# Row maxima of attention scores, reduced one head or two heads at a time

## The reference

```python
def attn(x, Wq, bq, Wk, bk, Wv, bv, Wo, bo):       # 32 heads of 16
    q, k, v = heads(x @ Wq + bq), heads(x @ Wk + bk), heads(x @ Wv + bv)
    probs = softmax(einsum('bhqd,bhkd->bhqk', q, k) / sqrt(16))
    return merge(einsum('bhqk,bhkd->bhqd', probs, v)) @ Wo + bo
def ffn(x, gate_w, up_w, down_w, gate_scale, up_scale, down_scale):   # 512 -> 1536 -> 512, weights rounded to fp8
    return qmm(silu(qmm(x, gate_w, gate_scale)) * qmm(x, up_w, up_scale), down_w, down_scale)
x = x + layernorm(attn(layernorm(x)))
x = x + layernorm(ffn(layernorm(x)))
```

## Time and profile before

| | |
|---|---|
| median of 3 runs | 1727.8 us (1726.58 to 1728.24) |
| the profiled execution, its own time | 1726.27 us |
| its span, first to last instruction | 1724.5 us |
| PE busy | 1584.0 us (92%) |
| DVE busy | 1192.2 us (69%) |
| ACT busy | 907.9 us (53%) |
| POOL busy | 600.8 us (35%) |

### The profile page before, as it was taken

How to read it: one execution, slowest core, us unless ns; L and a number is a source line. 1 busy time by engine, 2 the same in 40 slices (tenths; PEclk the granted TensorE clock), 3 DMA queues, 4 the chain that set the end, 5 groups by cost and what they waited for, 6 DMA issues and landing times.

```text
span 1724.5 us, 22880 instructions
## 1 busy us (share of the span) xinstructions
PE 1584.0 (92%) x8266; PEld 734.5 (43%) x8266; DVE 1192.2 (69%) x2200; ACT 907.9 (53%) x1624; POOL 600.8 (35%) x504
## 2 busy tenths in 40 slices
PE   4898999999999989999989999979999999999996
PEld 3433433334344333333333433314555555555553
DVE  6688888888878978888888887863354254354343
ACT  3177677666857757757766675663222222222221
POOL 4124343533632642533453362143422222222221
PEclk9799999999999999999999999969999999999998
DMA  3312122221312312212221121420121021021110
GB/s 116 86 50 69 41 58 58 83 58 42 102 32 66 99 38 58 88 50 63 64 82 50 38 84 50 141 77 25 37 74 56 19 74 49 25 73 50 49 49 25
DMA packets 81740, 105.63 MB, mean 61 GB/s; under 512 B 16214, under 2 KB 46934, under 8 KB 81624
## 3 DMA queue, kind: packets, MB, share of 16 engines
q1 hardware_dynamic: 81628, 104.17, 20.2%
HBM read 52.71 MB, written 21.50 MB: 43 GB/s over the span
## 4 chain that ended last, share of the span: by engine, by line
PE 63%; DVE 21%; ACT 7%; issue 5%; DMA 3%; SPq 1%; POOL 1%; POOLq 0%; ACTq 0%; DVEq 0%
PE ring L1357 19%; PE side L996 14%; PE down_sums L1371 10%; DVE maxima L827 9%; PE contexts L1070 8%; PE scores L1058 6%; PE maxima_scores L1035 4%; ACT probs L733 3%; DVE channel_shift_bits L964 1%; DVE channel_shift_bits L962 1%; DVE denominators L852 1%; DVE y L818 1%; DVE ctx_raw L857 1%; DVE qkT L811 1%; ACT qkT L660 1%
## 5 line engine op out<-in xcount | busy, mean ns | idle before, releaser
L827 DVE TENSOR_REDUCE maxima<-maxima_scores 128x1 f32<-128x512 f32 x1024 | 655.5, 680 | 106.1 <-PE maxima_scores L1035 102.3
L733 ACT ACTIVATE probs<-scores 128x512 f32<-128x512 f32 x1024 | 550.2, 602 | 301.4 <-PE scores L1058 300.1
L1035 PE MATMUL maxima_scores<-k_stack,q_stack 64*128 64x512 f16 x1024 | 338.8, 388 | 53.2 <-DVE maxima L827 53.0
L1058 PE MATMUL scores<-q_stack,k_stack 64*128 64x512 f16 x1024 | 326.7, 389 | 19.1 <-ACT probs L733 13.2
L1070 PE MATMUL contexts<-probs,v_one 128*32 128x512 f32 x2048 | 277.5, 614 | 17.7 <-ACT denominators L677 12.8
L1314 DVE SCALAR_TENSOR_TENSOR fuse<-ring,up_scale,gate 128x512 f32<-128x512 f32 x96 | 72.0, 750 | 289.2 <-PE ring L1357 280.5
L1228 POOL TENSOR_TENSOR fuse_low<-fuse,fuse_high 128x512 fp32r<-128x512 f32 x96 | 122.9, 1281 | 381.1 <-ACT fuse_high L1250 381.1
L1058 PEld LDWEIGHTS scores<-q_stack,k_stack 64*128 64x128 f16 x1024 | 67.0, 94 | 338.5 <-ACT probs L733 190.0
L1371 PE MATMUL down_sums<-down_q,fuse_high 128*128 128x512 f32 x384 | 166.7, 434 | 1.8 <-POOL fuse_low L1228 1.0
L1250 ACT CAST fuse_high<-fuse 128x512 fp32r<-128x512 f32 x96 | 59.6, 621 | 203.8 <-DVE fuse L1314 162.8
L1246 ACT ACTIVATE gate<-ring,gate_scale 128x512 f32<-128x512 f32 x96 | 66.0, 687 | 176.7 <-PE ring L1357 176.7
(11 more groups left out here) (196 smaller groups left out, 2431.1 us busy)
## 6 DMA issues: line engine op xcount, KB each, us to landing
q_stack<-qkT SPq DMA_DIRECT2D x192, 64.0 KB, 2.0
k_stack<-qkT SPq DMA_DIRECT2D x192, 64.0 KB, 2.0
x_rows<-in_L_attn_hidden_states SPq DMA_DIRECT2D x8, 1024.0 KB, 5.6
x_residual<-in_L_attn_hidden_states SPq DMA_DIRECT2D x32, 256.0 KB, 2.9
middle_rows<-y SPq DMA_DIRECT2D x32, 256.0 KB, 3.3
x_rows_ffn<-middle_rows SPq DMA_DIRECT2D x8, 1024.0 KB, 5.7
x_residual_ffn<-middle_rows SPq DMA_DIRECT2D x8, 1024.0 KB, 7.9
out_rows<-y_ffn SPq DMA_DIRECT2D x32, 256.0 KB, 2.2
```

Of the source, the lines that this page charges most:

```text
L733: act.activation(probs[:, n % 2, j, :], work[(b * (GH * STEPS) + GH * n + j) % RING][:], ACT.Exp, scale=float(D) ** -0.5).then_inc(p_full, 1)
L827: dve.tensor_reduce(maxima[:, g % 2, at:at + 1], bank[:], AX.X, ALU.max).then_inc(rot_free, 1)
L1035: mm = pe.matmul(bank[:], q_st[half, s, qc * P:qc * P + P], k_st[half, s, :], start=True, stop=True)
L1058: mm = pe.matmul(work[i % RING][:], k_st[half, s, c * P:c * P + P], q_st[half, s, :], start=True, stop=True)
```

## The change

One DVE instruction reduces two heads. A slot of the ring `maxima_scores` is now two banks (`[P, 2, S]`), and the ring has two slots. PE writes the two heads of a pair into them with two products, the odd head (e = 1) and then the even one. Only the first of a pair waits for the slot two items back, and only the second raises `rot_full`. DVE then reduces 128 x 2 x 512 to 128 x 2 in one `tensor_reduce`. There are 512 such reductions in place of 1024. So that PSUM's eight banks suffice, `scores` has two banks in place of three, so that a score product waits for the exponential two before it. The transposes "x", "t" and "f" use one bank of a slot and hold the whole slot. What DVE does between the reductions is tied to the first or second pair where it was tied to the first, second or third head. The amounts of lead, of products and of exponentials are as before.

```diff
-LEAD = 28
-RING = 3
+LEAD = 14
+RING = 2
@@
-    rot = [ps(f"maxima_scores{i}", [P, S]) for i in range(RING)]
+    rot = [ps(f"maxima_scores{i}", [P, 2, S]) for i in range(RING)]
     work = [ps(f"scores{i}", [P, S]) for i in range(RING)]
@@
-    MAXIMA = NH * T
+    PAIRS = NH * T // 2
+    HALF = GH * T // 2
     def maximum(i):
-        g, k = divmod(i, GH * T)
-        return "s", g, k // (2 * T) * 2 + 1 - k % 2, k // 2 % T
+        g, k = divmod(i, HALF)
+        return "s", g, k // T, k % T
@@
-        lo = LEAD + n * T
-        out = [(maximum(i % MAXIMA), b + i // MAXIMA) for i in range(lo, lo + T) if b + i // MAXIMA < B]
-        if lo % (GH * T) == 0:
+        lo = LEAD + n * 2
+        out = [(maximum(i % PAIRS), b + i // PAIRS) for i in range(lo, lo + 2) if b + i // PAIRS < B]
+        if lo % HALF == 0:
@@
-                _, g, j, qc = item
-                at = j % 2 * 2 * T + j // 2 * T + qc
+                _, g, u, qc = item
                 dve.wait_ge(rot_full, p + 1)
-                dve.tensor_reduce(maxima[:, g % 2, at:at + 1], bank[:], AX.X, ALU.max).then_inc(rot_free, 1)
+                both = maxima[:, g % 2, :].rearrange("p (e m) -> p e m", e=2)[:, :, u * T + qc]
+                dve.tensor_reduce(both, rot[p % RING][:], AX.X, ALU.max).then_inc(rot_free, 1)
@@
                     if k == 0 and before:
                         take(before[1], before[0])
-                    if k == 1 and before and before[0][0] == "o":
+                    if k == 0 and before and before[0][0] == "o":
@@
-                    if n % 8 == 0 and n and k == 1:
+                    if n % 8 == 0 and n and k == 0:
                         denominators_odd(b, n // 8 - 1)
-                    if n % 8 == 0 and n and k == 2:
+                    if n % 8 == 0 and n and k == 1:
                         contexts_odd(b, n // 8 - 1)
@@
-            if p >= RING:
+            if p >= RING and (item[0] != "s" or e == 1):
                 pe.wait_ge(rot_free, p - RING + 1)
@@
-            mm.then_inc(rot_full, 1)
+            if item[0] != "s" or e == 0:
+                mm.then_inc(rot_full, 1)
@@
                         if beside:
-                            rot_item(items[j][1], items[j][0])
+                            rot_item(items[u][1], items[u][0], 1 - j % 2)
```

More of the change, by code:

```diff
@@ L300, in attention_pass @@
     SIDES = len(side_order)
-    START_BANKS = (side, cps, work[2])
+    START_BANKS = (side, cps, work[1])
     b_square = xT_l[0:1, 0:2, :]
@@ L897, in _ @@
         weight_low("v")
-        reductions(0, 5)
+        reductions(0, 3)
         take(0, ("q", 1))
@@ L903, in _ @@
         take(0, ("v", 0))
-        reductions(5, 10)
+        reductions(3, 5)
         take(0, ("v", 1))
-        reductions(10, 16)
+        reductions(5, 8)
         take(0, ("v", 2))
-        reductions(16, LEAD)
+        reductions(8, LEAD)
         dve.wait_ge(const_a, CONSTS)
@@ L940, in turn @@
                         take(before[1], before[0])
-                    if k == 1 and before and before[0][0] == "o":
+                    if k == 0 and before and before[0][0] == "o":
                         dve.wait_ge(side_free, side_at[before] + 1)
                         stats("out", y, before[0][1])
-                    if n in (1, 2) and k in (1, 2) and not last:
-                        t = 2 * (n - 1) + k - 1
+                    if n in (1, 2) and k in (0, 1) and not last:
+                        t = 2 * (n - 1) + k
                         if t == 0:
@@ L948, in turn @@
                         stats("in", x_rows, t)
-                    if n == 3 and k == 1 and not last:
+                    if n == 3 and k == 0 and not last:
                         moments("in", b + 1)
-                    if n == 18 and k == 1 and b:
+                    if n == 18 and k == 0 and b:
                         moments("out", b - 1)
+                    if n % 8 == 0 and n and k == 0:
+                        denominators_odd(b, n // 8 - 1)
                     if n % 8 == 0 and n and k == 1:
-                        denominators_odd(b, n // 8 - 1)
-                    if n % 8 == 0 and n and k == 2:
                         contexts_odd(b, n // 8 - 1)
@@ L1022, in side_piece, with rot_item @@
                 mm.then_inc(side_full, 1)
-        def rot_item(n, item):
+        def rot_item(n, item, e=0):
             p = rot_at[item, n]
-            bank = rot[p % RING]
-            if p >= RING:
+            bank = rot[p % RING][:, e, :]
+            if p >= RING and (item[0] != "s" or e == 1):
                 pe.wait_ge(rot_free, p - RING + 1)
             if item[0] == "s":
-                _, g, j, qc = item
-                if j == 1 and qc == 0:
+                _, g, u, qc = item
+                if e == 1 and u == 0 and qc == 0:
                     pe.wait_ge(stack_in[g % SETS], filled(n, g))
-                s = (g % SETS) * 2 + j // 2
-                half = slice(64 * (j % 2), 64 * (j % 2) + 64)
-                mm = pe.matmul(bank[:], q_st[half, s, qc * P:qc * P + P], k_st[half, s, :], start=True, stop=True)
+                s = (g % SETS) * 2 + u
+                half = slice(64 * e, 64 * e + 64)
+                mm = pe.matmul(bank, q_st[half, s, qc * P:qc * P + P], k_st[half, s, :], start=True, stop=True)
             elif item[0] in "xf":
@@ L1087, in maxima_products @@
             for part, n in rot_start(lo, hi):
-                rot_item(n, part)
+                for e in (1, 0) if part[0] == "s" else (0,):
+                    rot_item(n, part, e)
         pe.wait_ge(const_a, SUMS)
```

26 lines of the change are left out of this document (13 added, 13 removed).

## The result

The changed kernel takes 1757.5 us (median of 3 runs, 1757.29 to 1758.18) against 1727.8 us: 1.0177 times the time before, 95% interval 1.0157 to 1.0197. It is slower by some 30 us; 1753 was forecast.

A forecast was written before the change was run, and what follows sets the result against it. No engine is full within attention; what counts is who is late for whom. Terms 4.8 + 0.6 + 0.5 - 1.9 - 0.7 make +3.3 us per middle turn, +24 to +25 in all: 1753 us, range 1712 to 1778.

The forecast's parts named there:

- The reduction itself: DVE's merged reduction of 1024 holds it 1.13 us where two held it 1.19; some 34 us of DVE saved.
- The take comes later: DVE's take of a side item waits for the whole pair, delaying PE's side matmuls 0.48 us; +4.8 us per turn.
- the ten steps: Steps 5, 7, 11, 13, 15, 19, 26, 28, 30, 31, each booked 0.48 us longer for the later take.
- Two score banks: Scores wait for exponentials: +0.48 us in steps 5, 11, 19, 26, not added to the take's; +0.6 for steps 20 to 25.
- Denominators: Odd contexts in steps 8, 16 and 24 are read half a pair later, delaying `contexts`; +0.5 us for all three.
- The ring of four banks: PE's waits at a pair's second product go, mainly in steps 0 to 4; step 5 starts earlier: -1.9 us per turn.
- The clock: Low clock behind step 0's wait, some 1.5 us in roughly half the turns, may go: -0.7 us per turn.
- The two ends: Before the first turn -0.5 us at most; first and last turns +2.5 us each.
- The sum: +3.3 us per middle turn, +19.8 for six, +5 for first and last turns, -0.5 before: +24 to +25.
- B: Rival, chance 0.24: faster, ring waits end and DVE's saving is felt while later takes stay hidden; 1690 to 1722 us.
- D: Rival without its own chance: two score banks alone decide, losing 0.15 to 0.48 us in all 32 steps; 1778 us.

The follow-up runs named there:

- e2: Kernel before with two score banks in place of three, maxima ring of three single banks untouched: 1.012, 1745.7 us.
- e3: Kernel before with two score banks and a maxima ring of four single banks, each head reduced by itself: 0.9929, 1711.2 us.
- e7: Changed kernel with each pair reduced by two instructions of one head, the take behind both: 1.022, 1763.4 us.
- e1: Changed kernel with DVE taking the finished side item before the first pair's reduction, not behind it: 0.995, 1716.1 us.
- e8: As e7, but the take of the side item between the two reductions of a step's first pair: 1.0058, 1735.4 us.
- e4: Kernel before with the take of the side item behind the second single reduction, not the first: 1.0208, 1759.4 us.
- e5: Kernel before with the take of the side item ahead of the first reduction, nothing else: 1.0209, 1761.5 us.
- f2: Changed kernel with the take ahead of the first pair for v and o items alone: 1.0062, 1734.9 us.

## Why the prediction was right, step by step

**The chain of single edits.** Read as ratios to the kernel before, from row to row:

| kernel | ratio | us added |
|---|---|---|
| before | 1 | |
| two score banks (e2) | 1.012 | +21 |
| fourth maxima bank (e3) | 0.9929 | -33 |
| a pair as one slot, two reductions, then the take (e7) | 1.022 | +50 |
| one instruction for both (the change) | 1.0177 | -7 |
| taken first instead (e1) | 0.995 | -39 |

(us added: difference of ratios by 1726.) The loss sits in the fourth row, which is more than one edit (slots in twos, the wait for both products, the take behind both, the denominators' later place). e1 and e8 show what most of it is. Moving the take ahead of the pair gives 39 us back; 21 of them return when only the second head's reduction is taken out from before it (e8 against the change: 1.0177 to 1.0058; 28 against e7, which has the same two instructions).

**The reduction itself: right.** 1.12 to 1.14 between starts in runs of pairs. The Trainium skill (VectorE: DVE Perf Modes, the section on the TRN2 errata) would have 1.19 for a row of 1024 elements; the row is 1.20 to 1.23, but the next starts 0.07 to 0.09 before its end. The busy time fell by 34 us, not by the 64 that this formula of the skill would give.

**The take comes later: right in kind, with luck in the sum.** For the ten steps I booked 4.8 us a turn. Measured growth of their lengths: 0.48 (5), 0.49 (7), 0.49 (11), 0.52 (13), 0.53 (15), 0.54 (19), 0.48 (26), 0.15 (28), 0.56 (30), 0.56 (31): 4.8. Not all of it is the take's. In 11, 19 and 26 it is the score banks' delay, as forecast, and with the take first (e1) they give nothing back, and 5 gives 0.27. Steps 7, 15, 30 and 31 give back 0.48 to 0.63. Two don't fit: 13 gives back 0.07 (0.25 of its 0.52 comes with two score banks, e2), and 28 gives back 1.12 where 0.48 was booked. Its growth is only 0.15 as other gains nearly cancel that (4.75 in e2 and e3). That these make 4.8 together is luck.

**Two score banks: right in the four steps, not in the stretch.** Forecast +0.48 in steps 5, 11, 19 and 26: 0.48 to 0.50 in e2. Steps 20 to 24 grew by 0.54 together, and 0.6 was booked for 20 to 25; but in e2, with the score banks alone, they shrank by 0.20. Only steps 20 and 21 (+0.10 and +0.16) are as told; the rest of the 0.54 came with the pairs, in step 22. The four steps make 2.0 us a turn. Of e2's growth of 20 us in span 13.4 lie in the six middle turns and 6.4 in the last turn and behind it, more than such steps explain.

**Denominators: the number came, the cause isn't shown.** Steps 8 to 10 and 16 to 18 changed by -0.06 together and step 25 by +0.61: +0.55 for the 0.5 booked. But in e3, which has neither pairs nor the later place, step 25 grew by 0.41, and PE's wait for the odd contexts is 14.3 us (2.3 before, 17.6 in the changed kernel). So most of that wait comes with the banks; no run moves the denominators alone.

**The ring of four banks: right kind, and nearly the size.** Steps 0 to 4 changed by -2.05, +0.56, -0.86, +1.48 and -0.10: -1.0, where -1.9 was booked. Step 0's wait went as told. Step 3 became 6.18 us long: DVE, behind from there on, reduced a whole pair (from 652.32) ahead of the take, and PE stood 1.96 us:

```profile
652.32 1.22 DVE L828 TENSOR_REDUCE maxima<-maxima_scores 128x2 f32<-128x1024 f32 x1
...
653.45 0.74 DVE L812 SCALAR_TENSOR_TENSOR qkT<-side,bias_qk,qkT 128x512 f16<-128x512 f32 x1
...
654.25 0.50 PE L997 MATMUL side<-xT_high,wk_high 128*128 128x512 f32 x1 [1.96 <-DVE qkT L812]
```

These medians hold the clock too. Steps 3 and 4 together, first in the third turn, then in the fifth (busy time of the engines; the granted clock is third from the end):

```profile
364.62:373.97 9.35, 7.47 (x46) 3.02 (x46) 8.49 (x16) 5.54 (x11) 4.85 (x5) 1.00 0.18 52
650.08:661.06 10.98, 9.02 (x46) 3.13 (x46) 8.65 (x16) 5.55 (x11) 4.83 (x5) 0.84 0.16 47
```

The same 46 matmuls take 1.6 us longer in the fifth turn, at 0.84 of the full clock, and 10.8 to 11.0 in every middle turn but the third. In the third turn, with full clock in both kernels, steps 0 to 4 changed by -1.33, +0.55, -0.84, +1.11 and -1.01: -1.5 for the -1.9. In e3, with the ring but without pairs, the medians of the five give -3.1: the pairs give back most of what the ring wins.

**The clock: the term that was wrong.** I booked -0.7 a turn for stretches of low clock that would vanish. The one behind step 0's wait did, but others came, in steps 3, 4 and 22. The third turn has none in either kernel. Before:

```profile
346.72:484.75 138.03, 127.64 (x732) 51.98 (x729) 117.85 (x216) 94.44 (x173) 57.64 (x48) 1.00 0.24 65
```

The changed kernel:

```profile
351.72:493.64 141.92, 124.91 (x733) 51.31 (x730) 114.53 (x152) 95.46 (x173) 57.40 (x48) 1.00 0.23 63
```

That is +3.9 us, where the forecast without its clock term is +4.0. Over the six middle turns the mean grew by 4.3 (139.0 to 143.3): the clock cost 0.4 a turn and gave nothing back. The stretch from 130 to 1110 us says the same; first the kernel before:

```profile
130.00:1110.00 980.00, 908.72 (x5161) 369.45 (x5160) 829.51 (x1510) 665.75 (x1221) 390.71 (x324) 0.99 0.23 64
```

The same stretch of the changed kernel:

```profile
130.00:1110.00 980.00, 866.89 (x4989) 350.96 (x4988) 778.61 (x1028) 650.21 (x1181) 386.16 (x323) 0.98 0.22 61
```

The mean granted clock is 0.98 of the full 2.4 GHz and was 0.99. The changed kernel is slower, so the stretch holds fewer of its matmuls, and PE is less busy (866.9 us for 908.7), but that does not explain the clock by itself. The same stretch of e7, with PE less busy still:

```profile
130.00:1110.00 980.00, 855.55 (x4979) 348.57 (x4979) 803.79 (x1466) 650.79 (x1182) 387.31 (x323) 1.00 0.22 61
```

So the clock isn't what makes pairs slow: with 1.00 of it e7 needs 143.4 us a middle turn, and e3, without pairs, 137.0. Which waits cost clock and which don't is left open; no run tried it. e7 has the wait of 1.9 us in step 3 too, and no low clock behind it.

**The two ends: both wrong, and they cancel by luck.** Before the first turn I booked -0.5; the first score product came 7.8 us earlier (68.8 us for 76.6). For the first turn I booked +2.5; it grew by 9.6, from 129.7 to 139.3. The gain before the first turn goes with the ring: the first scores come at 75.6 to 76.6 in the kernels with three single maxima banks (before, e2, e4, e5) and at 68.8 to 71.5 in all with four banks. In the kernel before, PE waited there with a projection queued behind:

```profile
55.35 1.20 PE L1035 MATMUL maxima_scores<-k_stack,q_stack 64*128 64x512 f16 x2 [3.13 <-DVE maxima L827]
56.49 0.79 PE L996 MATMUL scores<-wv_high,xT_high 128*128 128x512 f32 x1
```

But PE's waits for the ring ahead of the first score are 6.7 us before and 6.6 in the changed kernel, so the time came by way of the clock as well. The same stretch before:

```profile
50.00:68.50 18.50, 14.04 (x40) 8.41 (x39) 9.50 (x18) 3.44 (x6) 4.97 (x4) 0.73 0.65 139
```

The changed kernel:

```profile
50.00:68.50 18.50, 11.43 (x55) 6.46 (x53) 14.97 (x21) 3.45 (x6) 4.97 (x4) 0.99 0.67 142
```

With 0.99 of the clock PE does 55 matmuls there, with 0.73 only 40; how much of that is clock and how much waits isn't told apart. In e3, with four banks and 0.82, the first score comes at 71.5.

The first turn's loss goes with the pairs (it is 131.0 us long in e3, 136.6 in e1) and in part with the clock. The first turn before:

```profile
76.65:206.33 129.68, 119.48 (x681) 45.44 (x680) 110.21 (x200) 89.69 (x166) 44.59 (x37) 0.98 0.20 54
```

The changed kernel:

```profile
68.81:208.07 139.26, 119.58 (x682) 45.03 (x680) 107.67 (x135) 90.93 (x166) 44.52 (x37) 0.95 0.19 51
```

An estimate from these rows: 0.05 of 139.3 less 0.02 of 129.7 is some 4 of the 9.6 us, if PE set the pace all through. Another part is a mechanism that I had not priced. The transpose "t" of a group's maxima needs a corner of one bank but holds a whole slot of two, and until DVE has read it the ring is one pair deep. The end of step 21 and step 22 of the fifth turn in the changed kernel (PE and DVE):

```profile
734.84 0.28 PE L1048 MATMUL maxima_scores<-ident,maxima 128*16 128x128 f32 x1
...
734.97 1.23 DVE L828 TENSOR_REDUCE maxima<-maxima_scores 128x2 f32<-128x1024 f32 x1 [0.38 <-PE maxima_scores L1036]
...
736.26 0.39 PE L1036 MATMUL maxima_scores<-k_stack,q_stack 64*128 64x512 f16 x2 [0.77 <-DVE maxima L828]
```

Behind the transpose PE waits until DVE has finished the pair ahead of it (734.97, done about 736.2). Step 22 is 3.76 us here, as in e1, and 2.88 in e3, which has no pairs (2.71 before); in the turns in which low clock falls on it, it is 4.59 to 5.24, so that the median is 4.17. Step 23 got 1.22 shorter, so steps 22 to 24 are only 0.2 longer than before at full clock (11.5 and 11.3; 10.2 in e3). In the first turn step 22 went from 2.71 to 5.03, clock included (3.76 in f2), and step 6 from 2.74 to 3.76. No run gave the transpose a slot of its own, so what this mechanism costs is argued, not shown.

**The sum.** Six middle turns +26.0 for +19.8, the first +9.6 and the last +3.2 for 2.5 each, the time before the first turn -7.8 for -0.5: +31.0, which is the growth of the span, where some +25 was forecast. At full clock the middle turns came to +3.9 for +4.0, though terms inside partly cancel; the 6 us that are missing are the clock, some +2.7 over six turns where -4.2 was booked. B's own sum is off a little: 40 off 1726 is 1686, under the 1690 to 1722 given with it. Of the rivals, B (faster) needed the takes hidden; e1 shows that the ring and the merged instruction do win once they are. D did not come: a plain step without a take (6) kept 3.67 us.

What stays open: whether a third score bank beside the pairs would win, as all eight banks are in use; what the denominators' later place and the slot held by a transpose cost by themselves; and which waits bring low clock.

## What to carry to other kernels

An instruction merged for throughput on an engine that isn't full also delays what is queued behind it: before merging, list who waits for the next instruction in that queue and how much cover he has (here 0.32 us, against a delay of 0.75), and put that instruction first, if it is ready in time: where it waits for another engine, as in e5, and the ring behind it is short, putting it first cost 2.1%. Count a ring in what it holds when a small item takes a slot, not in banks. And PSUM banks are worth what their waits are worth: moving one bank from the scores to the maxima won 0.7%, with the take in the right place 1.6%, while the merged instruction, for which the banks had been rearranged, gave 0.4% by itself.

## What the runs showed of the hardware

Two DVE reductions that stand next to each other overlap by 0.07 to 0.09 us at both lengths: 512 elements last 0.68 and start 0.60 apart, 1024 last 1.20 to 1.21 in such a run and start 1.12 to 1.14 apart. So merging two of them saves some 0.07 us (34 us of busy time over 512 pairs).

A short stretch of low clock costs nearly as much as the wait ahead of it: in steps 3 and 4 PE waits 1.96 us for a take in the fifth turn, and the two steps, with the same work, last 10.98 us at 0.84 of the full clock and 9.35 at full clock.
